# The rotation of the third layer moved from the attention steps to the end of the slot

## The reference

```python
# each of the three layers
xn = _ln(x) * (1 + sc_msa) + sh_msa
q, k, v = split(xn @ w_qkv + b_qkv)          # layers 1 and 3 also normalise q and k by head
attn = softmax(q @ k.T * HD ** -0.5)
x = x + g_msa * ((attn @ v) @ w_proj + b_proj)
xn2 = _ln(x) * (1 + sc_mlp) + sh_mlp
x = x + g_mlp * (gelu(xn2 @ w1 + b1) @ w2 + b2)
# after the third layer; U is 288 x 64, R a 64 x 64 rotation of each batch
U, _ = qr(P); R = expm(A(silu(cond) @ W.T + b))
z = einsum('btn,nd->btd', x, U)
z_rot = einsum('btd,bde->bte', z, R)
x_rot = x + einsum('btd,nd->btn', z_rot - z, U)
```

## Time and profile before

| | us |
|---|---|
| median of 3 runs (5078.34 to 5092.95) | 5081.57 |
| the profiled execution | 5082.07 |
| its span | 5080.3 |
| third layer, first to last rotation add | 3536.2 to 5077.2 |

### The profile page before, as it was taken

One profiled execution on the slowest core, in us unless ns is written; L12 is line 12 of the kernel. 1 busy time (PEld: TensorE's weight loads), 2 busy tenths in 40 slices (PEclk: granted clock), 3 DMA queues, 4 the chain that ended last, 5 costly groups with the idle time before them and its releaser, 6 DMA issues. The chain is left out here.

```text
span 5080.3 us, 125326 instructions
## 1 busy us (share of the span) xinstructions
PE 4506.7 (89%) x46073; PEld 3767.7 (74%) x46073; DVE 3663.6 (72%) x7723; ACT 2273.7 (45%) x3828; POOL 1139.6 (22%) x2044
## 2 busy tenths in 40 slices
PE   6654899999999986999999999958999999999998
PEld 4543688888888875888888888757777777777776
DVE  5665788888888864676676676657777777777774
ACT  0111555555555534555554554424444444444443
POOL 1001222222222222222222222212222222222221
PEclk7576899999999997999999999978999999999999
DMA  3001100101010011101101000010000000000000
GB/s 71 20 1 41 35 25 28 28 28 28 28 28 28 26 35 44 29 28 28 28 28 28 28 28 27 22 51 23 23 25 22 25 22 25 22 25 22 25 20 18
DMA packets 122230, 141.59 MB, mean 28 GB/s; under 512 B 14446, under 2 KB 117780, under 8 KB 122112
## 3 DMA queue, kind: packets, MB, share of 16 engines
q1 hardware_dynamic: 121968, 139.75, 10.0%
q10 hardware_dynamic: 144, 0.22, 0.0%
HBM read 110.87 MB, written 29.06 MB: 28 GB/s over the span
## 5 line engine op out<-in xcount | busy, mean ns | idle before, releaser
L867 DVE TENSOR_REDUCE mx<-S 128x4 f32<-128x1024 f32 x768 | 920.5, 1217 | 80.3 <-PE S L1105 77.4
L629 ACT ACTIVATE pT<-S 128x1024 f32<-128x1024 f32 x768 | 745.3, 1022 | 366.5 <-PE S L1131 362.3
L577 ACT ACTIVATE hf<-M 128x512 f32<-128x512 f32 (+1 forms) x480 | 266.7, 556 | 1159.8 <-PE M L1185 672.4
L504 POOL TENSOR_SCALAR hh<-hf 128x512 fp32r<-128x512 f32 (+1 forms) x480 | 280.4, 584 | 1170.0 <-ACT hf L577 1127.2
L1131 PE MATMUL S<-qT,kT 32*128 32x256 f32 x9216 | 427.9, 296 | 64.8 <-ACT pT L629 63.4
L1105 PE MATMUL S<-kT,qT 32*128 32x256 f32 x3072 | 370.9, 336 | 84.3 <-DVE mx L867 45.9
L1131 PEld LDWEIGHTS S<-qT,kT 32*128 32x128 f32 x9216 | 331.2, 185 | 137.0 <-ACT pT L629 91.8
L1144 PE MATMUL A<-pT,V 128*32 128x256 f32 x6144 | 414.7, 388 | 19.5 <-ACT pT L629 19.5
L858 DVE TENSOR_TENSOR hl<-hf,hh 128x512 fp32r<-128x512 f32 (+1 forms) x480 | 323.8, 676 | 114.0 <-POOL hh L504 112.0
L1185 PE MATMUL M<-xh,w_hi 128*128 128x256 f32 x1728 | 393.7, 310 | 3.3 <-POOL xh L480 3.3
L1105 PEld LDWEIGHTS S<-kT,qT 32*128 32x128 f32 x3072 | 224.1, 189 | 206.2 <-DVE mx L867 82.1
(11 more groups left out here) (229 smaller groups left out, 10151.8 us busy)
## 6 DMA issues: line engine op xcount, KB each, us to landing
mid<-xbo SPq DMA_DIRECT2D x64, 288.0 KB, 3.2
xld<-mid SPq DMA_DIRECT2D x64, 288.0 KB, 3.0
xa<-mid SPq DMA_DIRECT2D x64, 288.0 KB, 3.5
gA<-gates SPq DMA_DIRECT2D x96, 144.0 KB, 3.3
gM<-gates SPq DMA_DIRECT2D x96, 144.0 KB, 3.0
xld<-in_x_dram SPq DMA_DIRECT2D x32, 288.0 KB, 3.5
xa<-in_x_dram SPq DMA_DIRECT2D x32, 288.0 KB, 3.5
out_dram<-xbo SPq DMA_DIRECT2D x32, 288.0 KB, 2.2
```

What stands on the lines that cost most here:

```text
L504: pool.tensor_scalar(hh[:, 2 * f:2 * f + m, :].rearrange("p m c -> p (m c)"), hf[:, f % 2, 0:m * T], 1.0, 0.0, ALU.mult, ALU.add).then_inc ...
L577: act.activation(hf[:, f % 2, 0:c], MBANK[f % 2][:, 0:c], ACT.Gelu if rot else ACT.Gelu_apprx_tanh).then_inc(s["m_hf"], 1)
L629: act.activation(pT[:, g % 2, 2 * h:2 * h + 2, :], S[:, 2 * h:2 * h + 2, :], ACT.Exp, scale=float(HD) ** -0.5).then_inc(s["a_ex"], 1)
L867: dve.tensor_reduce(mx[:, p, :, :], S[:, r:r + 2, :].rearrange("p a (t k) -> p a t k", t=NT), AX.X, ALU.max).then_inc(s["a_mx"], 1)
```

## The change

It concerns the third layer alone. Its steps now stand in the order that layers 1 and 2 use: `down1` in three pieces, `M_turn` before `A_pv(a, 3)`, `M_up_first` straight after `A_turn_o`, `M_xf`, `M_xh` and `M_xl` before the steps of the attention behind which they stood. The rotation of `d` moves to the end of the slot, between the QKV products of `nxt`, and uses one MLP bank, MBANK[0], for its whole chain: `R_turn` in two parts with `R_x` between them, since both parts write the same columns. `R_turn(d, 0)` waits for the last gelu of `m`. The copies go to `xf` (the attention's) in place of `xf2`. `R_out` writes two score banks, behind the seventh `A_max`, and `R_x3` adds from there as the last step of DVE's slot; the next slot's `A_scoresT(a, 0)` waits for it. SP's code is not changed. (Indentation cut by 20 columns.)

```diff
@@ -521,3 +521,3 @@
         A_xh(nxt)
-    if m is not None and not rot:
+    if m is not None:
         M_xh(m)
@@ -528,4 +528,2 @@
     if m is not None:
-        if rot:
-            M_xh(m)
         M_hh(m, 0)
@@ -549,4 +547,2 @@
     wait(act, "m_hl", n, 0)
-    if rot:
-        wait(act, "r_z", n - first, 0)
     for c in range(KC):
@@ -563,2 +559,4 @@
         wait(act, "a_xl", n, 0)
+        if rot:
+            wait(act, "r_z", n - first - 4, 0)
     if c != 1:
@@ -637,8 +635,11 @@
 
-def R_x(n):
+def R_x(n, part, nxt):
     b = n - first
-    wait(act, "r_T", b, 1)
-    act.activation(xf2[0:KP, 0:2, :].rearrange("p m c -> p (m c)"), MBANK[1][0:KP, :], ACT.Identity).then_inc(s["r_x"], 1)
-    wait(act, "r_T", b, 2)
-    act.activation(xf2[0:KP, 2, :], MBANK[0][0:KP, 0:T], ACT.Identity).then_inc(s["r_x"], 1)
+    if part == 0 and nxt is not None:
+        wait(act, "a_xl", nxt, 1)
+    wait(act, "r_T", b, part + 1)
+    if part == 0:
+        act.activation(xf[0:KP, 0:2, :].rearrange("p m c -> p (m c)"), MBANK[0][0:KP, :], ACT.Identity).then_inc(s["r_x"], 1)
+    else:
+        act.activation(xf[0:KP, 2, :], MBANK[0][0:KP, 0:T], ACT.Identity).then_inc(s["r_x"], 1)
 
@@ -646,3 +647,3 @@
     wait(act, "r_z", n - first, 1)
-    act.activation(zT[:, :], MBANK[1][0:ROT, 0:T], ACT.Identity).then_inc(s["r_zs"], 1)
+    act.activation(zT[:, :], MBANK[0][0:ROT, 0:T], ACT.Identity).then_inc(s["r_zs"], 1)
 
@@ -671,7 +672,3 @@
         A_xf(nxt, 2)
-    if rot and d is not None:
-        R_x(d)
-        R_z(d)
-        R_y(d)
-    if m is not None and not rot:
+    if m is not None:
         M_xf(m)
@@ -684,6 +681,2 @@
         high_m(act, layer, range(KC, NCH))
-    if m is not None and rot:
-        M_xf(m)
-    if a is not None and rot:
-        A_ohi(a)
     if m is not None:
@@ -691,3 +684,3 @@
         M_gelu(m, 1)
-    if a is not None and not rot:
+    if a is not None:
         A_ohi(a)
@@ -700,2 +693,3 @@
         load_table(p, 0, ACT.Exp)
+    turns = rot and d is not None
     if nxt is not None:
@@ -704,5 +698,14 @@
         A_qkv(nxt, 0)
+    if turns:
+        R_x(d, 0, nxt)
     if nxt is not None:
         A_qkv(nxt, 1)
+    if turns:
+        R_x(d, 1, nxt)
+        R_z(d)
+    if nxt is not None:
         A_qkv(nxt, 2)
+    if turns:
+        R_y(d)
+    if nxt is not None:
         A_qkv(nxt, 3)
@@ -933,3 +936,3 @@
         wait(dve, "r_o", n - first, i + 1)
-        dve.tensor_tensor(xo[:, i, :], MBANK[1 - i][:, 0:D], xo[:, i, :], ALU.add).then_inc(s["r_x3"], 1)
+        dve.tensor_tensor(xo[:, i, :], S[:, i, 0:D], xo[:, i, :], ALU.add).then_inc(s["r_x3"], 1)
 
@@ -976,5 +979,3 @@
         A_oraw(a, 1)
-    if d is not None and rot:
-        R_x3(d)
-    if m is not None and not rot:
+    if m is not None:
         M_xl(m)
@@ -986,4 +987,2 @@
         A_max(p, 0)
-    if m is not None and rot:
-        M_xl(m)
     if a is not None:
@@ -1016,2 +1015,4 @@
         A_negmax(p)
+    if d is not None and rot:
+        R_x3(d)
     if a is None and m is not None and layer < LAYERS - 1:
@@ -1119,2 +1120,4 @@
         wait(pe, "a_nmc", n, 1)
+        if rot:
+            wait(pe, "r_x3", n - first - 2, 0)
         wait(pe, "a_klo", n, 2)
@@ -1168,4 +1171,2 @@
         wait(pe, "a_xf", nxt, 3)
-    if rot:
-        wait(pe, "r_x3", n - first, 0)
     wait(pe, "m_x2", n, 0)
@@ -1228,12 +1229,14 @@
 
-def R_turn(n, p=None):
-    wait(pe, "m_x2", n, 2)
-    if p is not None:
-        wait(pe, "a_xf", p, 3)
-    for c in range(KC):
+def R_turn(n, part, p):
+    if part == 0:
+        wait(pe, "m_x2", n, 2)
+        if p is not None:
+            wait(pe, "m_hf", p, 5)
+    else:
+        wait(pe, "r_x", n - first, 1)
+    for c in ((0, 1), (2,))[part]:
         for i in range(NT):
-            op = pe.transpose(MBANK[1 - c // 2][0:KP, (c % 2) * T + i * P:(c % 2) * T + (i + 1) * P],
+            op = pe.transpose(MBANK[0][0:KP, (c % 2) * T + i * P:(c % 2) * T + (i + 1) * P],
                               xo[:, i, c * KP:(c + 1) * KP], ident[:, :])
-        if c:
-            op.then_inc(s["r_T"], 1)
+    op.then_inc(s["r_T"], 1)
 
@@ -1243,3 +1246,3 @@
     for k in range(KC):
-        op = pe.matmul(MBANK[1][0:ROT, 0:T], U[:, k, :], xf2[0:KP, k, :], start=(k == 0), stop=(k == KC - 1))
+        op = pe.matmul(MBANK[0][0:ROT, 0:T], U[:, k, :], xf[0:KP, k, :], start=(k == 0), stop=(k == KC - 1))
     op.then_inc(s["r_z"], 1)
@@ -1253,6 +1256,8 @@
 
-def R_out(n):
+def R_out(n, p):
     wait(pe, "r_ys", n - first, 1)
+    if p is not None:
+        wait(pe, "a_mx", p, PAIRS - 1)
     for i in range(NT):
-        pe.matmul(MBANK[1 - i][:, 0:D], yT[:, i * P:(i + 1) * P], UT[:, :], start=True, stop=True).then_inc(s["r_o"], 1)
+        pe.matmul(S[:, i, 0:D], yT[:, i * P:(i + 1) * P], UT[:, :], start=True, stop=True).then_inc(s["r_o"], 1)
 
@@ -1292,4 +1297,2 @@
         A_pv(a, p, 0)
-        if rot:
-            down1(16, 27)
     if nxt is not None:
@@ -1297,4 +1300,3 @@
     if a is not None:
-        if not rot:
-            down1(16, 22)
+        down1(16, 22)
         A_scoresT(a, 2)
@@ -1304,12 +1306,7 @@
     if a is not None:
-        if not rot:
-            down1(22, 27)
+        down1(22, 27)
         A_scoresT(a, 3)
-    if rot and d is not None:
-        R_turn(d, nxt)
     if a is not None:
         A_pv(a, p, 2)
-    if rot and d is not None:
-        R_z(d)
-    if m is not None and not rot:
+    if m is not None:
         M_turn(m, nxt)
@@ -1323,10 +1318,5 @@
         A_turn_qk(p)
-    if rot and d is not None:
-        R_out(d)
     if a is not None:
         A_turn_o(a)
-    if m is not None and rot:
-        M_turn(m, nxt)
-    if not rot:
-        first_up()
+    first_up()
     if a is not None:
@@ -1348,10 +1336,21 @@
         pe.wait_ge(w_lo, NCH * (layer + 1))
+    turns = rot and d is not None
     qkv(0)
+    if turns:
+        R_turn(d, 0, m)
     qkv(1)
+    if turns:
+        R_turn(d, 1, m)
     down0(0, 8)
     score(6)
+    if turns:
+        R_z(d)
     qkv(2)
     score(7)
+    if turns:
+        R_y(d)
     qkv(3)
     down0(8, 16)
+    if turns:
+        R_out(d, p)
     qkv(4)
```

## The result

The changed kernel takes 5156.6 us (median of 4 runs, 5149.7 to 5158.6) beside 5080.0 us of the kernel before on the same chip: a ratio of 1.0143, 95% interval 1.0123 to 1.0163. It is slower by 1.4%. The forecast was 5126 us, range 5066 to 5165. The profiled execution has a span of 5154.4 us, against 5080.3: 74.1 us more.

The account below looks back on a forecast made before the run. TensorE's order (PE busy 89%) was taken as the bound. 27 third-layer slots going from 51.2 to 53.2 us gave +54, the edges -9: +45 us on 5082.1, hence 5126 us, range 5066 to 5165.

Parts of the forecast that it names:

- The bound and the base: TensorE's order sets the pace; third-layer slot built from the first layer's 42.5 us, less 1.1 of waits, plus 4.0 of rotation.
- Wait 1: Third layer, TensorE at `R_turn(d, 0)` waits for the last gelu: 1.95 us a slot, not much below 1.5.
- wait 2: Third layer, TensorE at `R_turn(d, 1)` waits for `R_x`, which follows the first QKV copy on ACT: 0.8 us a slot.
- Wait 3: Next xld load queues behind the store awaiting `R_x3`; DVE stands 3.5 us, of which 3.25 reach TensorE, mainly at `M_turn`.
- Without any fall of the clock: Third-layer slot with all three new waits but no clock loss: 51.4 us, against 51.2 before the change.
- the term that was mis-sized: Clock loss in each third-layer slot: 1.2 us behind `R_turn` plus 0.6 behind `M_turn`, together 1.8, between 0 and 3.4.
- Rival C: Both low-clock stretches cost in full, or a third comes: slots of 54.6 us and more, 5165 us and up; chance 0.10.
- two low stretches in most slots: Sign of being right: TensorE's clock falls to half level in two stretches in most third-layer slots.
- That waits this short cost no clock: Reading of the Trainium skill, which names longer gaps: clock term nil, third-layer slot 51.4 us; the prediction spoke against it.
- rival A: Waits only, clock loss as before: third-layer slots of 50.8 to 51.9 us, 5078 us in all; chance 0.18.
- The edges: Four slots at the third layer's edges have no late load and gain 2 to 3 us each: -9 us (0 to -16).
- B: The load's delay doesn't reach TensorE, as DVE has slack ahead of `M_turn`: slot 49.5 us, 5027 us; chance 0.09.

## Why the prediction was right, and where it was off

*The bound and the base* held: the third layer has the first layer's slot plus the rotation once nothing is waited for, 45.3 measured against 45.4.

*Wait 1* was 1.81 us (forecast 1.95) and *wait 2* 0.71 (0.8), both from rows of another layer. Removing them took the slot from 51.4 to 48.6 with the clock aside, 2.8 us for 2.5 of waits.

*Wait 3*, the load behind the store, is the step that decided the sign. 4.16 us from the add's end to `A_stats` (forecast 4.14), 3.73 us on VectorE, and 48.2 us for the shortest slot without it against 51.4 with it: 3.2 us (forecast 3.25). It is shown from both sides, by taking it out of the new order and by putting it into the old one.

*Without any fall of the clock* a slot has 51.4 us, as the sum said. So the three waits eat all of the gain of 3 us and the 1.7 us that the clock lost before, and what makes the change slower is the clock: 53.94 - 51.4 = 2.5 us a slot. This is **the term that was mis-sized**: I took 1.8. The two places were right, one low stretch behind `M_turn` and one behind `R_turn`, and so was the price of each in the earlier trace rows: 53.0 us where one comes, 54.5 where both do. Of 27 slots 10 had two short ones and 11 had one, 10 x 3.1 + 11 x 1.6 = 49 us, which is what 27 x 1.8 had forecast. What I had not in the sum are the long stretches: two slots of 57.5 us, 6.1 each, and one of 58.6, 7.2, or 19 us. Rival C had named "a third" low stretch, not a long one. That the short ones came to the 49 us is in part luck: behind `M_turn` I had taken one slot in three, and 16 of 27 had the fall, while behind `R_turn` 16 had a short one where 1.2 of 1.7 us had meant 19. And two low stretches in most slots, which I had named as a sign of being right, came in 11 of 27 only.

*That waits this short cost no clock* would have given slots of 51.4 us and a time near that of before (rival A, 5078 us). The time is 5156.6, and the granted clock fell to the half level behind a wait of 2.20 us, and behind two of 1.81 and 0.71 us with work between them. The Trainium skill ("TensorE: Matmul & The Clock Gate", section "Why this matters for your kernels") warns there only of longer gaps than these. The measurement decides: these shorter ones were enough.

*The edges* were -9 in the forecast and -4.1 in the layer as measured, but as a sum of two parts, -13.6 in front and +9.5 behind, of which I had not foreseen the second. In front the better order won as forecast (10.3 us, and 3.3 that are not the order's). Behind, I gave the last slots the same gain; but they have no QKV products, and the rotation stands bare behind the last gelu:

```profile
5051.42 0.85 PE L1239 MATMUL M<-ident,xbo 128*96 128x128 f32 x4 [3.02 <-ACT hf L575]
...
5098.14 0.61 PE L1239 MATMUL M<-ident,xbo 128*96 128x128 f32 x4 [2.65 <-ACT hf L575]
...
5127.75 0.61 PE L1239 MATMUL M<-ident,xbo 128*96 128x128 f32 x4 [2.22 <-ACT hf L575]
```

Behind the first of these waits the clock stays low for 17 us:

```profile
5051.50:5068.50 17.00, 15.95 (x55) 11.14 (x55) 7.25 (x15) 3.28 (x7) 1.36 (x4) 0.50 0.09 21
```

The kernel with the early load has the same three waits and no stretch of that length there, and needs 137.8 us behind the last full slot where the changed kernel needs 143.0. So some 5 of the 9.5 us are owed to that stretch. The other 4 I put down to the three waits, less what the better order gives; no run separates the two.

*The rivals.* B (faster, 5027 us, since the lateness doesn't reach TensorE) did not happen, but its time is nearly that of the kernel whose load is early, 5022 us: the price was right, the condition was not met. A needed the clock to cost nothing more; 3 slots of 27 did that.

Together: +72.9 where 54 was forecast, -4.1 instead of -9, and +5.3 ahead of the layer's first negated maximum, where the change does nothing.

## What to carry to other kernels

When a step is moved to the end of a loop's turn, list what its completion releases on every queue, and what stands behind that in the same queue: here a store that waited for the moved step held the next load, in code that the change never touched, and one reordering of two transfers was worth 2.6%. A step placed behind a late one inherits its chain: before moving work behind an activation, find what the activation waits for and pull that forward. And price a wait of TensorE of one or two microseconds at its length plus the clock: here 2.5 us of waits cost 4.7 us a slot.

## What the runs showed of the hardware

The slot of the kernel before settled at 51.2 us, with one low stretch of the clock at the same place in each, while the same work in the new order spread over 51.4, 53.1, 54.6 and 57.5 us, with no fall, one, two, or a long one. The same two waits, of 2.20 and of 1.81 us, were followed by a fall in 16 and in 19 of 27 slots. With 1.9 us of work added the commonest slot was still 54.6 to 54.8 us, but now with one fall in place of two. Whether a turn's length settles at certain values, or the two sums only happen to agree (51.4 + 1.9 + 1.6 = 54.9), no run here decides. In either case a sum of waits holds only for turns at full clock (51.4 and 45.3 us measured, 51.4 and 45.4 forecast), and a small edit in a loop whose clock falls may show too little or too much. I had not expected low stretches of 10 to 17 us at a nearly fully occupied TensorE, either: in 15 us it was busy 14.4 us, at a granted clock of 0.54.
